# The beginning of a fused attention and mixture kernel rebuilt: how scales are spread, k ahead of q, both in halves

## The chip, the cores and the metric

One core of a Trainium2 chip runs the whole kernel. The metric is the device time of one execution in microseconds (us), as the median of several. Five engines work beside each other, each through its own list in order: TensorE (PE in the profile; matrix products and transposes, weight loads as PEld), VectorE (DVE), ScalarE (ACT), GpSimd (POOL) and SyncE (SP), which only issues transfers. They meet at semaphores alone.

## What is computed

For each of 4 batches of 512 tokens with 256 features, two adaptive layers follow each other. The modulation has six columns of features (shift, scale and gate for either layer).

```python
mod = (_silu(L0_c) @ L0_wmod).reshape(4, 6, 1, -1)
h = _layernorm(x) * (1 + ca) + sa
q, k, v = (h @ (codes * repeat(scales, 32, axis=0)) + bias  for each of q, k, v)   # 256 x 2048
attn = softmax(q @ k.T / sqrt(128))          # 16 heads of 128
x = x + ga * ((attn @ v) @ wo + bo)
h = _layernorm(x) * (1 + cb) + sb
x = x + gb * (h @ W.T + lora_of_the_two_best_of_8_experts(h))
```

The weights of q, k, v and o are stored as codes, and one scale holds for 32 rows of a column. For the change it matters that a scale has to reach the 32 partitions that hold its rows.

## The kernel before

The kernel is written engine by engine, and the order on each engine is the order of the text. Products are made with float32r numbers in two parts (high and low): `three` issues three products for one. So each operand needs a high part, made by ScalarE, and a low part, made by VectorE or GpSimd: h (`hT_hi`, `hT_lo`), the weights (`parts`), q, k, v, the probabilities (`pT_hi`, `pT_lo`) and the output of attention.

The 16 heads go in 8 pairs, and each pair runs 8 steps (2 heads for each of 4 batches), so there are 64 steps. `pair` stands once in every engine's list, and is called with `first=True` for steps 0 to 7, in a loop, and with `last=True`. In a step n TensorE makes the scores of n into four banks of PSUM (`score_ps`), the weighted sum of step n-2, the projections of q and k for step n+1, the output product, and the projection of v for n+1. VectorE makes the row maxima, 32x32 turns of the probabilities (`turn`, into `pB`), the low parts and the additions to `y_acc`. ScalarE makes the exponentials and high parts. SyncE moves the turned blocks by 16 transfers a step into `pT32` (L327), which starts when all four turns of the step are done (`pB_ok`). GpSimd makes the low parts of the probabilities (L404) and the weights of the next pair.

What comes ahead of step 0 is the place of the change:

- SyncE loads the condition, x of batch 0 (two halves), the modulation weights, then `load_first` for q and k: the codes and, in 4 transfers each (L291), the scales with every row read 32 times. x of batch 1, v, x of batch 2, o, x of batch 3 and the rest of the modulation weights follow.
- TensorE transposes the condition, keeps busy with 20 transposes of the unit matrix (L1111), makes the modulation columns of both chunks of features (L1117), transposes the normalised x of batch 0 (L1129), then 14 unit transposes more (L1136), the projection of q, that of k, and 10 unit transposes (L1164).
- VectorE makes the silu, the statistics of batch 0, its normalisation `z` (L805), the product of q's codes and scales (L843), the parts of h chunk by chunk (L811, L816), the biases and the statistics of batch 1.
- GpSimd makes the products for k and v (L377) and all `parts` of weights.
- ScalarE makes the exponential of the silu, the modulated h (`hT32`, L548), the high parts of q (L559) and k (L563), and normalises batch 1 (L586).

In step 0 VectorE's order is: four maxima (L941), turns 0 and 1 (L954), v's low part (L868), turns 2 and 3, the reciprocal, then the low parts of q (L857) and k (L862) for step 1 with the statistics of batch 2 in between, and the high parts of batch 1. `q_ok`, `k_ok` and `v_lo_ok` are what TensorE waits for.

## Time and profile before

| what | value |
|---|---|
| time, median of 3 runs | 777.58 us (777.32 to 777.62) |
| the profiled execution's own time | 777.42 us |
| its span | 775.5 us |
| busy: TensorE, VectorE, ScalarE, GpSimd | 766.5, 647.5, 517.6, 483.4 us |
| TensorE's granted clock, mean | 0.998 |
| transfers | 71898 packets, 90.67 MB |

The span is what the trace covers, from the first to the last recorded work. Times in the rows count from its start. A line of a timeline has the start, the time that the group took, the engine, the line of the kernel, the operation and its tiles (out<-in); "x4" means four instructions merged, and in brackets stands how long the engine had been idle and what ended that. TensorE's durations overlap, so from one start to the next is the better measure there.

### The profile page before, as it was taken

The page shows a single profiled execution, that of the slowest core. Times are in us where ns is not written, and L with a number is a line of the kernel's source. Part 1 is how long each engine was busy: PE and PEld are TensorE (multiplying, and loading weights), DVE is VectorE, ACT ScalarE, POOL GpSimd, SP SyncE. Part 2 cuts the span into 40 slices and gives each one's busy share as a digit, 9 for nine tenths or more (in the row PEclk, how much of TensorE's full clock was granted, in tenths as well). Part 3 has the DMA queues.
Part 4 walks back from the last instruction along what each step waited for, and adds up shares of the span by engine and source line. Part 5 has one row for each costly group of instructions (what it writes and reads, how often), then busy time and mean ns, then how long its engine had stood idle before and what let it go on. Part 6 is the DMA issues. An engine that isn't in the chain of part 4 may idle for free.

```text
span 775.5 us, 14722 instructions
## 1 busy us (share of the span) xinstructions
PE 766.5 (99%) x4206; PEld 667.7 (86%) x4206; DVE 647.5 (83%) x1254; ACT 517.6 (67%) x1124; POOL 483.4 (62%) x454
## 2 busy tenths in 40 slices
PE   7999999999999999999999999999999999999998
PEld 6888888888888888888888888888888888888887
DVE  5889888888888888888888888888898888879876
ACT  2788676667666676667666766676667676766841
POOL 4686576548655675556657575655667476789722
PEclk9999999999999999999999999999999999999999
DMA  7554355444454335444445434543355334433202
GB/s 216 162 154 124 95 147 150 139 107 99 118 144 131 95 96 139 129 124 98 110 133 147 98 94 122 146 125 95 96 145 152 95 94 107 112 89 86 56 1 109
DMA packets 71898, 90.67 MB, mean 117 GB/s; under 512 B 19574, under 2 KB 37431, under 8 KB 71867
## 3 DMA queue, kind: packets, MB, share of 16 engines
q1 hardware_dynamic: 53184, 74.00, 37.3%
q10 hardware_dynamic: 18682, 16.30, 7.0%
q8 instruction: 15, 0.25, 0.1%
q14 instruction: 17, 0.13, 0.1%
HBM read 22.06 MB, written 2.11 MB: 31 GB/s over the span
## 4 chain that ended last, share of the span: by engine, by line
PE 95%; POOL 1%; DVE 1%; DMA 1%; ACT 1%; SPq 1%; issue 0%; DVEq 0%
PE score L1102 9%; PE score L1103 9%; PE score L1104 9%; PE qv L1102 8%; PE qv L1103 8%; PE qv L1104 8%; PE o L1102 7%; PE o L1104 7%; PE o L1103 7%; PE ky L1102 4%; PE ky L1103 4%; PE ky L1104 4%; PE y L1102 2%; PE y L1104 2%; PE y L1103 2%; DMA stage<-in_L_attn_wk_scales_dram 1%
## 5 line engine op out<-in xcount | busy, mean ns | idle before, releaser
L404 POOL TENSOR_TENSOR pT_lo<-pT,pT_hi 128x512 fp32r<-128x512 f32 x248 | 314.6, 1305 | 240.7 <-ACT pT_hi L576 240.6
L660 ACT ACTIVATE prob<-score,neg_max 128x512 f32<-128x512 f32 x256 | 172.7, 688 | 79.7 <-DVE neg_max L941 79.5
L941 DVE TENSOR_REDUCE neg_max<-score 128x1 f32<-128x512 f32 x256 | 159.7, 682 | 1.6 <-PE score L1104 1.6
L954 DVE STREAM_TRANSPOSE pB<-prob 128x512 f32<-128x512 f32 x252 | 156.4, 678 | 0.0
L576 ACT ACTIVATE pT_hi<-pT 128x512 fp32r<-128x512 f32 x248 | 135.3, 620 | 0.0
L1102 PE MATMUL score<-k_hi,q_hi 128*128 128x512 f32 x256 | 101.2, 395 | 0.6 <-DVE k_lo L862 0.6
L1103 PE MATMUL score<-k_lo,q_hi 128*128 128x512 f32 x256 | 100.3, 392 | 0.0
L1104 PE MATMUL score<-k_hi,q_lo 128*128 128x512 f32 x256 | 99.7, 389 | 0.0
L1102 PE MATMUL o<-pT_hi,v_hi 128*128 128x512 f32 x248 | 96.6, 389 | 0.0
L1104 PE MATMUL o<-pT_hi,v_lo 128*128 128x512 f32 x248 | 96.5, 389 | 0.0
L1103 PE MATMUL o<-pT_lo,v_hi 128*128 128x512 f32 x248 | 96.5, 389 | 0.0
L857 DVE SCALAR_TENSOR_TENSOR q_lo<-qv,vecT,q_hi 128x512 fp32r<-128x512 f32 x64 | 47.9, 749 | 43.5 <-ACT q_hi L559 43.5
L862 DVE SCALAR_TENSOR_TENSOR k_lo<-ky,vecT,k_hi 128x512 fp32r<-128x512 f32 x64 | 48.0, 750 | 32.5 <-ACT k_hi L563 32.3
L559 ACT ACTIVATE q_hi<-qv,bias_now 128x512 fp32r<-128x512 f32 x64 | 44.2, 690 | 45.6 <-PE qv L1104 45.6
L563 ACT ACTIVATE k_hi<-ky,bias_now 128x512 fp32r<-128x512 f32 x64 | 44.2, 690 | 42.8 <-PE ky L1104 42.8
L1102 PE MATMUL qv<-wv_hi,hT_hi 128*128 128x256 f32 x252 | 71.6, 284 | 0.0
L1103 PE MATMUL qv<-wv_lo,hT_hi 128*128 128x256 f32 x252 | 71.3, 283 | 0.0
L1104 PE MATMUL qv<-wv_hi,hT_lo 128*128 128x256 f32 x252 | 71.3, 283 | 0.0
L571 ACT ACTIVATE o_hi<-o 128x512 fp32r<-128x512 f32 x63 | 37.8, 599 | 44.5 <-PE o L1104 42.3
L868 DVE TENSOR_TENSOR v_lo<-qv,v_hi 128x512 fp32r<-128x512 f32 x63 | 43.5, 691 | 27.2 <-ACT v_hi L567 27.0
L1104 PEld LDWEIGHTS score<-k_hi,q_lo 128*128 128x128 f32 x256 | 48.1, 188 | 10.5
L1102 PEld LDWEIGHTS score<-k_hi,q_hi 128*128 128x128 f32 x256 | 48.3, 189 | 9.1 <-issue 0.8
(262 smaller groups left out, 1824.7 us busy)
## 6 DMA issues: line engine op xcount, KB each, us to landing
pT<-pB SPq DMA_DIRECT2D x1008, 64.0 KB, 2.0
out_dram<-x_nat SPq DMA_DIRECT2D x8, 256.0 KB, 2.1
stage<-in_L_attn_wv_codes_dram ACTq DMA_DIRECT2D x7, 256.0 KB
stage<-in_L_attn_wv_scales_dram ACTq DMA_DIRECT2D x14, 128.0 KB
stage<-in_L_attn_wq_codes_dram ACTq DMA_DIRECT2D x7, 256.0 KB
stage<-in_L_attn_wq_scales_dram ACTq DMA_DIRECT2D x14, 128.0 KB
stage<-in_L_attn_wk_codes_dram ACTq DMA_DIRECT2D x7, 256.0 KB
stage<-in_L_attn_wk_scales_dram ACTq DMA_DIRECT2D x14, 128.0 KB
```

The source lines that it names most:

```text
L404: pool.tensor_tensor(split(pT_lo, kt), turned(par, kt), split(pT_hi, kt).bitcast(f32), ALU.subtract).then_inc(p_lo_ok, 1)
L559: act.activation(q_hi[:, :], qv_ps[:, :], ACT.Identity, bias=bias_now[:, 0, j:j + 1]).then_inc(q_hi_ok, 1)
L563: act.activation(k_hi[:, :], ky_ps[:, :], ACT.Identity, bias=bias_now[:, 1, j:j + 1]).then_inc(k_hi_ok, 1)
L576: act.activation(split(to, kt), turned(par, kt), ACT.Copy).then_inc(p_hi_ok, 1)
L660: act.activation(prob[:, i], score_ps[i][:, :], ACT.Exp, bias=neg_max[:, i:i + 1], accum_out=row_sum[:, s % 2, i:i + 1]).then_inc(exp_ok, 1)
L857: dve.scalar_tensor_tensor(out=q_lo[:, :], in0=qv_ps[:, :], scalar=bias[:, 0, head], in1=q_hi[:, :].bitcast(f32), op0=ALU.add, op1=ALU.sub ...
L862: dve.scalar_tensor_tensor(out=k_lo[:, :], in0=ky_ps[:, :], scalar=bias[:, 1, head], in1=k_hi[:, :].bitcast(f32), op0=ALU.add, op1=ALU.sub ...
L941: dve.tensor_reduce(neg_max[:, i:i + 1], score_ps[i][:, :], AX.X, ALU.max, negate=True).then_inc(max_ok, 1)
L954: dve.transpose(pB[:, s % 2, :, i].rearrange("p g k q -> p k g q"), prob[:, i].rearrange("p (k g q) -> p k g q", k=QT, g=G)).then_inc(pB_o ...
L1102: pe.matmul(dst, a_hi, b_hi, start=first, stop=False)
L1103: pe.matmul(dst, a_hi, b_lo, start=False, stop=False)
L1104: return pe.matmul(dst, a_lo, b_hi, start=False, stop=last)
```

## The change

The scales of q, k and v come as rows: `load_rows` on ScalarE's queue moves the 4 scale rows of each half of the features into 4 partitions of a tile that VectorE has zeroed (`rows_zero`), and TensorE spreads them over 128 partitions in PSUM by a product with a 0/1 matrix `block_rows` (`spread_rows`), padded with zeros to 128 partitions. VectorE multiplies codes and scales for all three, reading the scales from PSUM (`first_product`). SyncE loads k's codes ahead of q's.

The modulation is made chunk by chunk into two banks, and the transposes of a chunk follow directly, tile by tile behind `z`. The projections of k and then q are made in two halves of tokens, each half in its own bank (`project_halves`), with high and low parts by halves. Of the 44 unit transposes 6 stay. The high part of chunk 1 of h and the biases go from VectorE to ScalarE. Batch 1 is normalised by VectorE inside step 0 (was ScalarE, ahead of it). In step 0 VectorE's order is new, and all statistics of batch 2 come after the step.

```diff
+        block_rows = pB[:, 0, 1, 0]
+        scale_rows = dict(q=gb_row[:, 0:2], k=gb_row[:, 2:4],
+                          v=pB[:, 0, 0].rearrange("p i k q -> p (i k q)").rearrange("p (c n) -> p c n", c=2))
...
+        def load_rows(queue, m):
+
+            src = bass.AP(SCALES[m].tensor, 0, [[FEAT, NB], [NB * FEAT, 2], [1, PW]])
+            queue.wait_ge(rows_zero, 1 + "kqv".index(m))
+            queue.dma_start(scale_rows[m][0:NB], src).then_inc(ld_rows[m], 16)
...
+            load_first(sp, "k")
             load_first(sp, "q")
-            load_first(sp, "k")
             load_x(1)
...
             inverse_std(0)
+            parts("k", 0, 0)
             parts("q", 0, 0)
-            product("k", 0)
-            parts("k", 0, 0)
+            parts("v", 0, 0)
             parts("q", 0, 1)
             inverse_std(1)
-            product("v", 0)
-            parts("v", 0, 0)
             parts("k", 0, 1)
...
+            load_rows(act, "k")
+            load_rows(act, "q")
+            act.wait_ge(c_tr, 1)
+            act.activation(c_exp[:, :], qv_ps[:, 0:B * DC], ACT.Exp, scale=-1.0).then_inc(c_exped, 1)
+
+            load_rows(act, "v")
...
             for c in range(DC):
+                modulation_out(c)
                 input_high(0, c, score_ps[2 + c])
+            act.wait_ge(h_ev, 2)
+            act.activation(hT_hi[:, 1, tokens(0)], hT32[:, 1], ACT.Copy).then_inc(h0_hi, 1)
...
-            q_high(1, 0)
-            k_high(1, 0)
-            normalise(1, range(QT))
+            def half_high(m, u):
...
+            for m in "kq":
+                for u in range(2):
+                    half_high(m, u)
...
+            for m in "kqv":
+                dve.memset(scale_rows[m], 0.0).then_inc(rows_zero, 1)
+            dve.memset(block_rows, 0.0).then_inc(block_zero, 1)
...
+            first_product("k")
+            first_product("q")
+            input_hi(0, 0)
+            input_lo(0, 0)
+            dve.wait_ge(ld_x[1], 16)
+            row_statistics(1, 0)
+            row_statistics(1, 1)
+            input_lo(0, 1)
+            first_product("v")
+            row_statistics(1, 2)
+            row_statistics(1, 3)
             dve.wait_ge(vec_ok, 2)
...
+            half_low("k", 0)
+            half_low("k", 1)
+            half_low("q", 0)
+            half_low("q", 1)
+            variances(1)
...
+                    elif start:
+                        normalise(1, range(2))
+                        turn(0)
+                        v_low(1, 0, 0, ky_ps)
+                        normalise(1, range(2, QT))
+                        q_low(n + 2, head_slice(p, s + 1))
+                        turn(1)
+                        k_low(n + 2, head_slice(p, s + 1))
+                        turn(2)
+                        turn(3)
+                        inverse()
+                        input_hi(1, 0)
+                        input_hi(1, 1)
+                        dve.wait_ge(ld_x[2], 16)
+                        statistics(2)
...
-            for i in range(20):
+            for i in range(6):
                 pe.transpose(score_ps[0][:, (i % QT) * P:(i % QT + 1) * P], ident[:, :], ident[:, :])
+
+            def spread_rows(m):
+                pe.wait_ge(block_ok, 1)
+                pe.wait_ge(ld_rows[m], 16)
+                for c in range(2):
+                    ins = pe.matmul(first_scales(m)[:, c], block_rows[:, :, :].rearrange("a b q -> a (b q)"), scale_rows[m][:, c],
+                                    start=True, stop=True)
+                ins.then_inc(rows_mm[m], 1)
+
+            spread_rows("k")
+            spread_rows("q")
...
+            for u in range(DC):
+                for i, j in enumerate((SA + u, CA + u)):
+                    for c in range(DC):
+                        ins = pe.matmul(mod_banks[u][:, i * B:(i + 1) * B], wmod_1[:, c, j * P:(j + 1) * P], silu[:, c],
+                                        start=(c == 0), stop=(c == DC - 1))
+                ins.then_inc(mod_mm, 1)
+                for t in range(QT):
+                    pe.wait_ge(z_ok, t + 1)
+                    ins = pe.transpose(INPUT_BANKS[0][u][:, t * P:(t + 1) * P], z[:, 0, t, u * P:(u + 1) * P], ident[:, :])
+                ins.then_inc(h_tr, 1)
...
+            pe.transpose(score_ps[1][:, 0:VECS], vec_raw[:, :], ident[0:VECS, 0:VECS]).then_inc(vec_tr, 1)
+            spread_rows("v")
+
+            def project_halves(m, mm):
 
                 for c in range(DC):
-                    if by_half:
-                        pe.wait_ge(h_lo, c + 1)
+                    pe.wait_ge(h_lo, c + 1)
+                    cut = (slice(None), c, slice(0, HD))
+                    for u in range(2):
+                        ins = three(half_banks[m][u][:, 0:S // 2], (w_hi[m][cut], w_lo[m][cut]),
+                                    (hT_hi[:, c, half_tokens(u)], hT_lo[:, c, half_tokens(u)]), c == 0, c == DC - 1)
+                        if c == DC - 1:
+                            ins.then_inc((half_mm[m], mm)[u], 1)
...
+            pe.wait_ge(w_ok["k"], 1)
+            pe.wait_ge(mod_ok, 4)
+            project_halves("k", k_mm)
             pe.wait_ge(w_ok["q"], 1)
-            project(qv_ps, "q", 0, 0, True).then_inc(q_mm, 1)
-            pe.wait_ge(w_ok["k"], 1)
-            pe.wait_ge(mod_ok, 2)
-            project(ky_ps, "k", 0, 0).then_inc(k_mm, 1)
-            for i in range(10):
-                pe.transpose(score_ps[0][:, (i % QT) * P:(i % QT + 1) * P], ident[:, :], ident[:, :])
+            project_halves("q", q_mm)
```

## Rows read from the trace of the kernel before

**Rows 1.** The page, first part: busy time and share of each engine.
```profile
PE 766.5 (99%) x4206; PEld 667.7 (86%) x4206; DVE 647.5 (83%) x1254; ACT 517.6 (67%) x1124; POOL 483.4 (62%) x454
```

**Rows 2.** Three stretches: PE, PEld, DVE, ACT, POOL busy; granted clock, DMA share, GB/s.
```profile
7.50:10.75 3.25, 2.71 (x24) 2.46 (x23) 1.67 (x4) 0.58 (x3) 0.40 (x1) 1.00 0.57 156
11.00:14.25 3.25, 3.25 (x15) 3.25 (x16) 3.18 (x5) 0.87 (x2) 2.02 (x3) 0.51 0.98 252
14.25:17.75 3.50, 2.01 (x9) 1.31 (x9) 2.39 (x13) 0.89 (x2) 3.27 (x5) 1.00 0.73 248
```

**Rows 3.** Transfers: KB and us to landing; batch 1's x by issue; ScalarE's last vector.
```profile
stage<-in_L_attn_wq_codes_dram SPq DMA_DIRECT2D x1, 256.0 KB, 4.6
vec_raw<-in_L_attn_bv_dram ACTq DMA_DIRECT2D x1, 8.0 KB, 3.4
...
L309 SPq DMA_DIRECT2D x_nat<-in_L_attn_x_dram x1: 427/427/427, 7.8 to 7.8; - x1
...
DMA to landing us min/median/max: 7.8/7.8/7.8
```

**Rows 4.** Timeline of VectorE ahead of step 0.
```profile
7.93 1.67 DVE L805 SCALAR_TENSOR_TENSOR z<-x_nat,mv,rstd 128x256 f32<-128x256 f32 x4 [1.22 <-POOL rstd L362]
10.77 0.69 DVE L843 SCALAR_TENSOR_TENSOR stage<-stage 128x512 f32<-128x512 f32 x1 [1.17 <-DMA stage<-in_L_attn_wq_scales_dram]
11.38 0.42 DVE L811 CAST hT_hi<-hT 128x512 fp32r<-128x512 f32 x1
11.84 0.98 DVE L816 TENSOR_TENSOR hT_lo<-hT,hT_hi 128x512 fp32r<-128x512 f32 x1
...
15.64 1.41 DVE L783 BATCH_NORM_STATS2 stats<-x_nat 128x6 f32<-128x256 f32 x4 [1.04 <-DMA x_nat<-in_L_attn_x_dram]
```

**Rows 5.** Timeline of GpSimd and ScalarE ahead of step 0.
```profile
14.01 1.56 POOL L377 TENSOR_TENSOR stage<-stage 128x512 f32<-128x512 f32 x1 [0.60 <-DMA stage<-in_L_attn_wk_scales_dram]
...
16.34 0.73 POOL L390 TENSOR_TENSOR wk_lo<-stage,wk_hi 128x256 fp32r<-128x256 f32 x1
...
18.81 0.69 ACT L563 ACTIVATE k_hi<-ky,bias_now 128x512 fp32r<-128x512 f32 x1 [2.40 <-PE ky L1104]
```

**Rows 6.** Timeline of TensorE: first score products of steps 0 and 1.
```profile
20.43 0.47 PE L1102 MATMUL score<-k_hi,q_hi 128*128 128x512 f32 x1 [0.56 <-DVE k_lo L862]
...
30.60 0.40 PE L1102 MATMUL score<-k_hi,q_hi 128*128 128x512 f32 x1
```

**Rows 7.** Timeline of VectorE in steps 0 and 1, and TensorE's v of step 1.
```profile
21.40 2.75 DVE L941 TENSOR_REDUCE neg_max<-score 128x1 f32<-128x512 f32 x4 [1.11 <-PE score L1104]
24.06 1.29 DVE L954 STREAM_TRANSPOSE pB<-prob 128x512 f32<-128x512 f32 x2
25.98 0.69 DVE L868 TENSOR_TENSOR v_lo<-ky,v_hi 128x512 fp32r<-128x512 f32 x1 [0.62 <-ACT v_hi L567]
...
37.52 0.71 DVE L857 SCALAR_TENSOR_TENSOR q_lo<-qv,vecT,q_hi 128x512 fp32r<-128x512 f32 x1
...
38.71 0.37 PE L1102 MATMUL qv<-wv_hi,hT_hi 128*128 128x256 f32 x1
```

**Rows 8.** Step 0's probabilities: issues, landing time, first high part, low parts.
```profile
27.91 8.43 SPq L327 DMA_DIRECT2D pT<-pB  x13
...
pT<-pB SPq DMA_DIRECT2D x4, 64.0 KB, 2.0
...
40.69 0.64 ACT L576 ACTIVATE pT_hi<-pT 128x512 fp32r<-128x512 f32 x1
...
41.41 5.04 POOL L404 TENSOR_TENSOR pT_lo<-pT,pT_hi 128x512 fp32r<-128x512 f32 x4 [5.26 <-ACT pT_hi L576]
```

**Rows 9.** Timeline of TensorE and VectorE at the end of step 2.
```profile
51.60 0.28 PE L1102 MATMUL qv<-wv_hi,hT_hi 128*128 128x256 f32 x1
52.13 0.74 DVE L862 SCALAR_TENSOR_TENSOR k_lo<-ky,vecT,k_hi 128x512 fp32r<-128x512 f32 x1
53.04 0.40 PE L1102 MATMUL score<-k_hi,q_hi 128*128 128x512 f32 x1
```

More of the change, by code:

```diff
@@ L283, in load_first, with first_scales, half_tokens @@
                 rows = CODES[m].rearrange("(h p) d -> p h d", p=P)[:, 0:2]
-                at, row, half = [BLK * a for a in range(NB)], D, NB * D
             else:
                 rows = CODES[m].rearrange("(c p) f -> p c f", p=P)[:, :, 0:PW]
-                at, row, half = [BLK * a for a in range(NB)], FEAT, NB * FEAT
             queue.dma_start(codes[m][:, :, :], rows).then_inc(ld_w_first[m], 16)
-            for a in range(NB):
-                src = bass.AP(SCALES[m].tensor, a * row, [[0, BLK], [half, 2], [1, PW]])
-                queue.dma_start(scales[m][at[a]:at[a] + BLK], src).then_inc(ld_w_first[m], 16)
+            if m == "o":
+                for a in range(NB):
+                    src = bass.AP(SCALES[m].tensor, a * D, [[0, BLK], [NB * D, 2], [1, PW]])
+                    queue.dma_start(scales[m][BLK * a:BLK * (a + 1)], src).then_inc(ld_w_first[m], 16)
+        def load_rows(queue, m):
+            src = bass.AP(SCALES[m].tensor, 0, [[FEAT, NB], [NB * FEAT, 2], [1, PW]])
+            queue.wait_ge(rows_zero, 1 + "kqv".index(m))
+            queue.dma_start(scale_rows[m][0:NB], src).then_inc(ld_rows[m], 16)
+        def first_scales(m):
+            return {"q": o_ps[0], "k": o_ps[1], "v": score_ps[0]}[m][:, :].rearrange("p (c n) -> p c n", c=2)
+        mod_banks = (ky_ps, qv_ps)
+        half_banks = dict(q=(qv_ps, o_ps[0]), k=(ky_ps, o_ps[1]))
+        def half_tokens(u):
+            return slice(u * S // 2, (u + 1) * S // 2)
         def split(t, kt):
@@ L393, in input_lo @@
                 for c in range(DC):
[L394 to L395 removed]
+                    if b == 1:
+                        pool.wait_ge(h_hi, c + 2)
                     else:
@@ L798, in statistics, with normalise @@
                 variances(b)
-            def normalise(i):
+            def normalise(i, tiles=range(QT)):
                 b = i % B
                 dve.wait_ge(ln_rstd, i + 1)
-                for t in range(QT):
+                for t in tiles:
                     dve.scalar_tensor_tensor(out=z[:, b % 2, t], in0=x_nat[:, b * QT + t], scalar=mv[:, b, t, 0:1],
@@ L813, in input_lo @@
             def input_lo(b, c):
-                dve.wait_ge(h_hi, DC * b + c + 1)
+                if c:
+                    dve.wait_ge(h0_hi, 1)
+                else:
+                    dve.wait_ge(h_hi, 1)
                 dve.tensor_tensor(hT_lo[:, c, tokens(b)], hT32[:, c], hT_hi[:, c, tokens(b)].bitcast(f32),
@@ L970, in pair @@
                         turn(1)
-                        if start:
-                            v_low(1, 0, 0, ky_ps)
                         turn(2)
@@ L1296, in pair @@
                     early = first and s < 2
-                    pe.wait_ge(q_ok, n + 1)
-                    pe.wait_ge(k_ok, n + 1)
+                    if start:
+                        pe.wait_ge(half_lo["k"], 1)
+                        pe.wait_ge(k_ok, 1)
+                        pe.wait_ge(vec_ok, 2)
+                    else:
+                        pe.wait_ge(q_ok, n + 1)
+                        pe.wait_ge(k_ok, n + 1)
                     for i in range(QT):
+                        if start and i % 2 == 0:
+                            pe.wait_ge((half_lo["q"], q_ok)[i // 2], 1)
                         if not start:
```

107 lines of the change are left out of this document (50 added, 57 removed).

## The prediction

> **What bounds the kernel now.** I read the page's busy shares first. TensorE works 99% of the span [rows 1], so a saving counts only where TensorE itself is late, and that is the beginning. The timeline of the beginning shows why. The scales of q, spread by 32-fold reads from memory, hold VectorE's first product until 10.77 [rows 4], and those of k hold GpSimd's until 14.01 [rows 5]. After k's product (1.56 us) come its parts and its projection; ScalarE makes the high part from 18.81 in 0.69 us [rows 5], VectorE the low part, and the first scores start at 20.43, those of step 1 at 30.60 [rows 6]. From there TensorE hardly pauses, but a gain at 20.43 reaches the end only if nobody behind it is late in turn. So the last views are those of the other engines in steps 0 to 2: how much slack do they have?
>
> Little. VectorE's low part of q for step 2 runs from 37.52 to 38.23, and TensorE goes on to v, which needs it, at 38.71 [rows 7]: slack 0.5. The probabilities of step 0 are moved by 16 transfers of SyncE, which start at 27.91, right behind VectorE's last turn; 13 are issued in 8.43 us (0.65 apart), so the sixteenth at 37.65, and a transfer lands 2.0 after its issue [rows 8]. All have landed at 39.65, and ScalarE makes their high parts from 40.69 [rows 8]: slack 1.04. From that instant on, VectorE's work of step 2 is a chain without a gap; its low part of k ends at 52.87, and step 3's scores need it at 53.04 [rows 9]: slack 0.17. So TensorE's gain lasts only as far as step 0's probabilities come earlier too.
>
> **The change part by part.**
> (a) Scales. SyncE issues 12 transfers fewer for q, k and v (8 ahead of batch 1's x); three small ones on ScalarE's queue take their place. The codes of k take q's place, whose landing was 4.6 behind the issue at 2.57, so 7.2 [rows 3]; q's follow at about 9. For the rows of scales the nearest transfers are ScalarE's vectors, the latest of which landed 3.4 after its issue [rows 3]. VectorE's zeroing ahead of them has no row: between 0.2, little more than nothing, and 0.69, its 512-wide product [rows 4]; I take 0.6, the latter being nearest in size. Three of them put k's issue at 1.4 and q's at 2.0, landing by 4.8 and 5.4. The spreading products of TensorE have no row either: 256 columns cost 0.12 in one pass [rows 9], so two products cost 0.24 at least and, with several passes at half the clock, up to some 1.8; I take 1.7. They take the place of 14 of 20 warm-up transposes ahead of the modulation. If q's end 0.6 behind the modulation weights' landing, the wait for z covers it.
> (b) VectorE. z ends at 7.93+1.67 = 9.6 [rows 4]; ScalarE has fewer issues ahead of the exponential, so 9.5. Then k's product 0.69 (10.2), q's 0.69 (10.9), high part of chunk 0, 0.42 (11.3; it waits for nothing, because the transposes of chunk 0 now follow z tile by tile), low part 0.69 to 0.98 [rows 4] (12.2), two statistics of 0.35 (12.9), low part of chunk 1 (13.7). ScalarE makes the high part of chunk 1 by 12.4, in time.
> The two statistics stand behind a new wait, for x of batch 1, with chunk 1's low part, v's product and all low parts of k queued behind it. Before, this x was issued at 7.8 and landed 7.8 later, 15.6 [rows 3]. Now it is issued at 3.5, behind 1.5 MB instead of 2. The landing of q's codes shows 1.25 MB in the 6.0 us from 1.2 to 7.2 [rows 3]; the 0.75 MB more (k's or q's codes and this x) take 3.6 at that rate: 10.8, ahead of 12.2. I take no wait.
> (c) GpSimd loses the products of k and v. k's parts (0.73 for the low one [rows 5], up to 0.3 more beside VectorE) are done by 11.9, q's by 13.3. Neither is late.
> (d) TensorE and its clock. v's spreading stands ahead of k's projection, about 11.0 to 12.7. The clock is the open cost. After the stretch 7.50 to 10.75, small products and transposes with 2.71 us busy, it was granted at 0.51 in 11.00 to 14.25, that is at 1.2 GHz. Behind that stretch, which was filled with transposes, it was back at 1.00, and it stayed there in 14.25 to 17.75 with only 2.01 of 3.50 us busy [rows 2]. The change leaves the first stretch as thin, but fills the second with v's spreading and k's projection, and the third is busier than before; so I expect the same pattern, slow from about 11 to 14 and 2.4 GHz behind it.
> The Trainium skill, "TensorE: Matmul & The Clock Gate", Part 4, says that transposes don't count as busy for the gate. By that rule the dropped transposes cost nothing and rival C has no ground; by rows 2 the clock rose behind little else than transposes, so the trace doesn't agree, and C keeps its chance.
> Twelve half-width products take 53.04-51.60 = 1.44 us [rows 9]. k's chunk 0 is hidden behind VectorE; chunk 1 runs 13.8 to 14.6, q's projection to 16.1, its first half done at 15.7. ScalarE's high part of a half costs between 0.35 (half of 0.69) and 0.69, 0.48 taken because part of the 0.69 is fixed; VectorE's low part the same. With 0.3 to 0.5 of handing over the first scores are at **17.2**, 3.2 earlier.
> (e) Step 0 on VectorE. z of batch 1 moves here from ScalarE: 1.67 [rows 4]. Up to the last turn there are four maxima 2.75, z 1.67, four turns of 0.645, the low parts of v 0.69, q 0.71 and k 0.74: 9.1 [rows 7, 9]. The first maximum starts 0.97 behind the first scores [rows 6, 7], and ScalarE's high parts of v and k cost some 0.3 of waiting. Last turn: 17.2+0.97+9.1+0.3 = 27.6, where it was 27.9. **Of 3.2 us, 0.3 is left at the turns**, for z and two low parts now stand ahead of them.
> (f) TensorE in steps 0 and 1. v's low part ends at 17.2+0.97+2.75+0.84+0.65+0.69 = 23.1; from there to step 1's scores it took 30.60-26.67 = 3.9 [rows 6, 7], so 27.0: 3.6 earlier. But VectorE now has in one block, from 27.6 on, the reciprocal 0.1, the high parts of batch 1 0.84, statistics of batch 2 2.1, v's low part 0.7, maxima and turns 2.5 each, reciprocal and q's low part 0.8: 37.1 at most (36.8 if short ones overlap), where it was 38.23. TensorE, 3.6 ahead with 0.5 of slack, waits there for some 2 us and keeps 1.7 to 1.9.
> (g) Step 0's probabilities. SyncE starts 0.3 earlier and all have landed at 39.35. ScalarE is free then, its modulation copies ahead of them following TensorE, and takes them at 39.35 instead of 40.69. GpSimd's low parts (5.04, from 0.7 behind [rows 8]) and VectorE's chain of step 2 follow by the same 1.3. SyncE has no pause up to step 1's last transfer and lands that only 0.3 earlier, which is just enough for ScalarE; from step 3 on everything moves alike.
>
> **The sum.** 0.3 at the turns and 1.04 of slack at the landing: **1.3 us**. The profiled execution took 777.42, a span of 775.5 and 1.9 around it, 0.16 below the median of 777.58. The span becomes 774.2, the time by the median **776.2**. Each 1 us at the first scores is 1 us here.
>
> **The rivals.**
> A. The forecast, 776.2 (775.4 to 777.0, first scores 0.8 either way). For it: the slacks of 1.04 and 0.17. Chance 0.55.
> B. The lead is kept: VectorE's pieces fit into its waits, or the first scores come near 16. Up to 3.5, 774.1. Against it: z adds 1.67 to a chain whose slack is 0.5. Chance 0.2.
> C. The clock doesn't come back at 14.3 without the 24 dropped transposes behind z. k's last chunk costs 0.7 more and q's projection 1.4, less 0.4 behind its first half; first scores 18.9, gain -0.4, 778.0. Chance 0.15.
> D. Slower: the wait for x of batch 1. If it lands at 15.6 as before, 3.4 behind VectorE's readiness at 12.2, the first scores are at 20.6, the last turn at 31.0, the landing at 42.75, where ScalarE took it at 40.69: 2.1 slower, 779.6. It costs from a landing at 12.2 on and turns the sign at 13.5. Chance 0.1.
>
> **How the numbers follow.** Under 0.2% (1.55 us) a measurement here can hardly tell a difference. Of A, 0.22 lies beyond 1.55 us; with B faster is 0.42. The rest of A (0.33) and C make the same 0.48. D is slower, 0.1. The range 774.3 to 778.2 takes in A, C and B down to near its end; it leaves out D and B's last part.
>
> **What would show it.** First scores near 17.2 at a clock of 1.00; the last turn of step 0 and SyncE's first move near 27.6; TensorE idle for about 2 us in step 1 for q's low part, and for some tenths in step 2 for VectorE or the probabilities. VectorE waiting for x behind 12.2 would mean D, a clock of 0.5 behind 14.3 C, a last turn ahead of 26.5 B.

## The result, and the profile after

The changed kernel takes **779.07 us** (median of 11; 777.06 to 781.72) where the kernel before, beside it, takes 777.62 (777.30 to 778.26). The ratio is 1.0022, interval 1.0013 to 1.0030: slower by 0.2%. The prediction of 776.2 was wrong in sign. And the times now spread over 4.7 us, where those of before spread over 1.0 here, and over 2.4 in the largest set of its executions (34, beside the run again). (Four single executions of over 1000 us, two of them of the kernel before, are left out of all ranges and medians.)

The profiled execution took 778.99, with a span of 777.2. First the page of the changed kernel:

```profile
span 777.2 us, 14702 instructions
PE 766.4 (99%) x4192; PEld 666.8 (86%) x4192; DVE 652.2 (84%) x1264; ACT 517.1 (67%) x1127; POOL 479.8 (62%) x450
```

TensorE's share is unchanged [rows 1], so the difference must again be sought where TensorE is late. Next, the windows of the beginning, in the columns of [rows 2]:

```profile
6.50:9.75 3.25, 1.92 (x14) 1.49 (x13) 2.07 (x5) 0.05 (x1) 1.03 (x1) 1.00 1.06 372
10.00:13.25 3.25, 3.25 (x16) 2.83 (x15) 2.78 (x6) 1.45 (x4) 2.97 (x4) 0.50 1.06 323
13.25:16.75 3.50, 3.50 (x14) 3.14 (x14) 2.29 (x5) 1.34 (x5) 1.06 (x2) 0.50 1.05 287
```

The granted clock is 0.50, that is 1.2 GHz, in two stretches; before it was slow in one and back at 1.00 in 14.25 to 17.75 [rows 2]. TensorE's timeline shows what ran in them:

```profile
8.61 1.05 PE L1201 MATMUL ky<-c_silu,y_acc 128*128 128x4 f32 x8 [1.33 <-DMA y_acc<-in_L_wmod_dram]
10.05 1.71 PE L1201 MATMUL qv<-c_silu,y_acc 128*128 128x4 f32 x8
12.92 2.07 PE L1189 MATMUL score<-pB 128*128 128x256 f32 x4
15.22 0.41 PE L1176 MATMUL ky<-hT_hi,wk_lo 128*128 128x256 f32 x1
15.43 0.41 PE L1174 MATMUL y<-hT_hi,wk_hi 128*128 128x256 f32 x1
19.50 0.47 PE L1174 MATMUL score<-k_hi,q_hi 128*128 128x512 f32 x1 [0.82 <-DVE q_lo L918]
```

The modulation weights landed 6.5 after their issue instead of 4.9, v's spreading took 2.07, and k's half-width products follow at 0.21 instead of 0.12. First scores at 19.50: 0.9 earlier than before [rows 6], 2.3 later than predicted. Now the other engines in steps 0 to 3, from their timelines:

```profile
12.77 0.74 DVE L826 BATCH_NORM_STATS2 stats<-x_nat 128x6 f32<-128x256 f32 x2
29.04 1.29 DVE L1024 STREAM_TRANSPOSE pB<-prob 128x512 f32<-128x512 f32 x2
30.36 0.61 SPq L351 DMA_DIRECT2D pT<-pB  x1
42.25 0.63 ACT L607 ACTIVATE pT_hi<-pT 128x512 fp32r<-128x512 f32 x1 [0.53 <-DMA pT<-pB]
54.55 0.43 PE L1174 MATMUL score<-k_hi,q_hi 128*128 128x512 f32 x1
```

VectorE finds x of batch 1 without a wait (rival D is out). The last turn of step 0 ends at 30.33, SyncE starts 2.45 later than before, ScalarE takes the high parts 1.56 later, now waiting for the landing [rows 8], and step 3's scores start 1.51 later [rows 9]. That is the whole difference of the medians (1.45).

One more observation carries much of what follows. In the profiled executions the scores of step 3 start 722.4 to 722.7 before the end of the span, in 12 of the 16 kernels here, before and after among them. In the other four (hold, fill_all, fill_z, late4) it is 723.1 to 723.4, and in just these ScalarE waits 1.30 to 1.65 for the landing of step 1's probabilities at about 52. So the start of step 3's scores, plus what is left of a wait of that length, sets the time (fill1's 0.77 costs nothing).

### The profile page after: what moved, and what is told of

Its sections match the earlier page's. It is cut to its first block, busy times and chain, and to the rows that moved or that the text cites. A ratio compares the mean times of both kernels' runs of the same rounds, so it can differ in the third digit from the quotient of the medians.

```text
span 777.2 us, 14702 instructions
## 1 busy us (share of the span) xinstructions
PE 766.4 (99%) x4192; PEld 666.8 (86%) x4192; DVE 652.2 (84%) x1264; ACT 517.1 (67%) x1127; POOL 479.8 (62%) x450
## 4 chain that ended last, share of the span: by engine, by line
PE 90%; DVE 4%; ACT 2%; SPq 1%; DMA 1%; POOL 1%; issue 1%; DVEq 0%
PE score L1174 9%; PE score L1175 9%; PE score L1176 9%; PE qv L1174 7%; PE qv L1175 7%; PE qv L1176 7%; PE o L1174 7%; PE o L1175 7%; PE o L1176 7%; PE ky L1174 4%; PE ky L1176 4%; PE ky L1175 4%; PE y L1176 2%; PE y L1174 2%; PE y L1175 2%; SPq L351 1%
```

## The experiments

All times of one row come from one profiled execution of that kernel, except for the median and the range. "Landed" is ScalarE's first high part of step 0's probabilities, "wait 1" its wait for those of step 1. A median stands for 10 to 12 executions, in z_act for 6 and in z_hi_act for 8; the kernel before was measured beside each set, 125 times in all.

| kernel | median (range) | first scores | SyncE's start | landed | wait 1 | scores of step 3 |
|---|---|---|---|---|---|---|
| before | 777.6 to 777.7 (776.6 to 779.5) | 20.43 | 27.91 | 40.69 | 0 | 53.04 |
| changed | 779.07 (777.1 to 781.7) | 19.50 | 30.36 | 42.25 | 0.16 | 54.55 |
| again | 779.65 (777.8 to 781.9) | 17.23 | 28.57 | 40.28 | 0 | 53.77 |
| hold | 778.91 (776.9 to 781.5) | 17.45 | 28.31 | 39.95 | 1.65 | 52.30 |
| fill_t | 778.87 (776.8 to 780.1) | 17.22 | 28.55 | 40.06 | 0 | 53.73 |
| fill_m | 778.17 (776.7 to 779.1) | 18.68 | 29.55 | 41.06 | 0 | 54.76 |
| fill1 | 778.37 (777.1 to 780.2) | 19.57 | 30.49 | 42.00 | 0.77 | 54.33 |
| fill_all | 777.30 (776.8 to 777.9) | 16.67 | 28.00 | 39.71 | 1.50 | 52.01 |
| turns | 777.16 (776.5 to 777.5) | 17.28 | 24.93 | 40.36 | 0 | 52.72 |
| bare | 777.95 (777.2 to 781.8) | 21.19 | 28.18 | 40.96 | 0 | 53.31 |
| late2 | 777.59 (777.1 to 779.2) | 20.05 | 28.20 | 40.31 | 0 | 52.67 |
| late4 | 778.58 (777.6 to 779.1) | 20.66 | 29.65 | 41.52 | 1.32 | 53.84 |
| z_act | **775.53** (774.9 to 775.8) | 17.23 | 24.89 | 38.77 | 0 | 51.13 |
| z_hi_act | 775.72 (775.5 to 776.1) | 17.87 | 25.52 | 39.40 | 0 | 51.76 |
| z_plain | 778.03 (774.8 to 780.9) | 19.48 | 27.08 | 40.75 | 0 | 53.13 |
| fill_z | 777.20 (776.0 to 777.9) | 17.72 | 28.09 | 40.03 | 1.30 | 52.37 |

### The beginning: landing or clock?

**again** is the changed kernel unaltered.

> The changed kernel itself once more, to see its spread and a second profile. Clock theory (T1): its times lie anywhere from 777 to 782 because TensorE's clock drops to 1.2 GHz in the beginning at another moment in each execution; the profile then shows first scores and the last turn of step 0 moving with the slow stretch, about 1 us for 1 us in the time. Rival (T2, transfers): the spread comes from when the modulation weights land (8.6 us in the profile of the changed kernel); then the clock's stretch would be the same and the landing another.

779.65, ratio 1.0022 (1.0011 to 1.0033). This execution was another one than the first: the clock is 1.00 from its first rise at 8.7 on (how that is read stands at z_plain below), and the first scores start at 17.23, as predicted, although the modulation weights landed nearly as late as in the first profile (6.3 behind their issue; the modulation began 0.15 earlier). So the clock is what costs most of the 2.3 there. (The landing isn't free: where the clock is kept, the first scores follow it from 8.1 on, 16.67 in fill_all with the modulation begun at 8.09, 17.23 in z_act with 8.33, 17.87 in z_hi_act with 9.00.) And yet this execution took 778.15, 0.8 less than the first profiled one and still some 2 more than predicted, and the median is no better. Its windows show why:

```profile
10.00:13.25 3.25, 3.05 (x21) 2.40 (x21) 2.69 (x5) 2.66 (x8) 3.09 (x4) 1.00 1.06 325
34.80:38.20 3.40, 2.68 (x17) 2.35 (x18) 2.93 (x6) 3.40 (x10) 0.00 (x0) 1.00 0.40 99
38.20:42.50 4.30, 4.30 (x28) 4.30 (x26) 2.61 (x10) 3.12 (x10) 1.51 (x2) 0.64 0.55 150
```

The clock fell later instead, in steps 1 and 2 (0.50 from about 39.4 to 42.8), behind a stretch in which TensorE waits 0.7 at a time and makes small modulation products. In TensorE's timeline, from v's projection to the scores of step 3:

```profile
37.78 0.39 PE L1174 MATMUL qv<-wv_hi,hT_hi 128*128 128x256 f32 x1 [0.72 <-DVE q_lo L924]
53.77 0.40 PE L1174 MATMUL score<-k_hi,q_hi 128*128 128x512 f32 x1
```

37.78 is 0.93 earlier than before [rows 7], 53.77 is 0.73 later than before.

**hold** keeps the queue free until the modulation weights have landed.

```diff
             load_first(sp, "q")
+            sp.wait_ge(ld_wmod, 16)
             load_x(1)
             load_first(sp, "v")
```

> The changed kernel, but SyncE waits for the modulation weights before it issues x of batch 1 and all that follows. T2 (crowding: seven large transfers issued within 4.6 us delay the modulation weights from 7.0 to 8.6 us): they land near 7.1, the transposes of chunk 1 and h follow 1.5 us earlier and the time falls by 1 to 1.5 us, to about 777.5. T1 (clock): the landing moves but the slow stretch still holds the projections of k and q, gain under 0.7 us, and the spread of the times stays some 4 us wide.

778.91, ratio 1.0016 (1.0006 to 1.0026), and the spread of 4.5 stays. The weights landed 6.0 behind their issue, not 4.9, and 6.0 is also what fill_all has without this wait. So crowding by the transfers issued behind q's codes isn't shown to delay the landing, and it explains hardly any of the time. In the profile the clock was slow for 3.4 us only, and yet ScalarE waits 1.65 for step 1's probabilities.

**fill_t** puts 6 unit transposes, **fill_m** two real products of 256 columns, into TensorE's wait for the modulation weights.

```diff
             spread_rows("q")
+            for i in range(6):
+                pe.transpose(score_ps[0][:, (i % QT) * P:(i % QT + 1) * P], ident[:, :], ident[:, :])
             pe.wait_ge(ld_wmod, 16)
```

```diff
             spread_rows("q")
+            for c in range(2):
+                pe.matmul(first_scales("v")[:, c], block_rows[:, :, :].rearrange("a b q -> a (b q)"), scale_rows["q"][:, c],
+                          start=True, stop=True)
             pe.wait_ge(ld_wmod, 16)
```

> The changed kernel with six unit transposes more between the spreading of q's scales and the wait for the modulation weights, where TensorE was idle 1.3 us. T1, with transposes counting as activity: the clock no longer falls at 10 us, the projections of k and q run at 2.4 GHz, the first scores come near 17.5 instead of 19.5, the time is about 777.0 and its spread shrinks below 1 us. If transposes do not hold the clock, it stays at 779 with the same spread. T2: no change in the time.

> The same place filled with two products of 256 columns (the spreading of q's scales repeated, its result is overwritten) instead of transposes. T1: if only real products hold the clock, this one comes to about 777.0 with a small spread and the one with transposes does not; if both hold it they are alike; at half clock the fill takes some 1.7 us, so the modulation may start 0.4 us late. T2: no change, or 0.3 us slower.

778.87 (ratio 1.0011, 1.0002 to 1.0019) and 778.17 (1.0005, 0.9996 to 1.0014). The 777.0 that I had expected of one or both didn't come. fill_t's profile has the beginning at 1.00 and first scores at 17.22, but 0.50 at 39.2 to 42.6; fill_m's has a slow stretch in both places, in the beginning from 12.8 to 16.2. Filling one place doesn't keep the other.

**fill1** fills step 1 instead, with six products of 512 columns into a bank that is free, and **fill_all** does both.

```diff
+            def keep_busy(count):
+                for _ in range(count):
+                    pe.matmul(o_ps[0][:, :], w_hi["q"][:, 0, 0:HD], hT_hi[:, 0, tokens(0)], start=True, stop=True)
...
                     if first and s == 1:
                         pe.wait_ge(ld_wmod2, 16)
                         pe.wait_ge(h_ev, DC * 2)
                         modulation_columns(0)
+                        keep_busy(3)
...
+                        if first and s == 1:
+                            keep_busy(3)
                         pe.wait_ge(q_ok, n + 2)
```

> The changed kernel with 3 products of 512 columns on TensorE in step 1 behind the first modulation columns, and 3 more ahead of its wait for VectorE's low part of q, where it stood idle 0.7 us each time (results unused). Dip theory (T3): in the second profile of the changed kernel the clock was at 1.2 GHz from 39.3 to 42.7, behind a stretch of waits and small products, and v, transposes and scores took 4.6 us from 37.8 on where the kernel before needed 3.2; so 1.4 us of the gain are given back there in many executions. With the fill the clock stays at 1.00 in steps 1 and 2 and the median falls by 0.7 to 1.4 us against the changed kernel, the slowest executions (781 to 782) stay. Rival (T1 alone, the beginning): no gain, as the beginning is untouched; 0.2 to 0.6 slower if the fill delays the projections.

> The fill in step 1 and the two products of 256 columns behind the spreading of q's scales together. T1 and T3 together: median 776.5 to 777, slowest below 778.5. If crowding of transfers were the cause of the spread, it would stay as wide as with neither.

fill1: 778.37 (1.0009, 1.0000 to 1.0018), 1.2 GHz at 9.2 to 16.0, none in step 1. fill_all: **777.30** (0.9995, 0.9986 to 1.0004), 0.3 above the range that I had expected, and the spread is 1.1. Six added products in step 1, some 1.6 us (in turns, below, 0.80 and 0.77 from the first of three to what follows), on an engine that is busy for 99% of the time, and two more ahead of it make the kernel 1.8 us faster and steady. The profile has no slow stretch behind the first rise, and the mean clock on record is 1.000 in all eleven executions, where the 22 of the changed kernel have 0.991 to 0.998. So the clock explains the slower median and nearly all of the spread. (The changed kernel and fill_all were not measured beside each other; against the kernel before beside each, the difference is 1.7, or 2.2 with again.) But first scores at 16.67 are 3.8 earlier than before, and of that 0.3 is left at the end, with an interval that includes zero. This is the next question.

**bare** asks the same of the kernel before: it leaves out the 14 and the 10 unit transposes behind z (L1136, L1164).

> The kernel before with the 14 and the 10 unit transposes behind the first input's transposes taken out, nothing else. T1: without them the clock stays low through the projections of q and k in many executions, median 0.5 to 1.5 us slower, spread 2 to 4 us as in the changed kernel. Rival (the transposes don't count for the clock): no change beyond 0.1 us.

777.95, where the kernel before beside it has 777.56; three of the ten executions took over 780, and the ratio is 1.0015 (1.0002 to 1.0027). The mean clock on record is 0.995 or less in seven of the ten and in none of the 114 executions of the kernel before in these rounds, which have 0.996 to 1.000. The windows of bare:

```profile
10.00:13.25 3.25, 2.04 (x9) 1.55 (x8) 2.08 (x4) 1.80 (x4) 1.34 (x2) 0.50 0.99 211
13.25:16.75 3.50, 3.05 (x6) 1.81 (x7) 3.43 (x8) 0.21 (x1) 3.15 (x4) 0.50 0.85 258
```

Without them the clock stays at 1.2 GHz from 9.5 to 19.7, where it was back by 14.25 [rows 2] and, in the profiles of late2 and late4 below, which keep the transposes, by 15.7 and 13.2. The first scores start at 21.19. The Trainium skill, "TensorE: Matmul & The Clock Gate", Part 4, says that a transpose doesn't count as busy for the gate. The trace doesn't agree: unit transposes held the clock up here.

### From the first scores to the end: what took the rest?

In fill_all, ScalarE's high parts of step 0 and step 1, and TensorE's start of step 3:

```profile
39.71 0.63 ACT L607 ACTIVATE pT_hi<-pT 128x512 fp32r<-128x512 f32 x1 [0.37 <-DMA pT<-pB]
51.48 0.63 ACT L607 ACTIVATE pT_hi<-pT 128x512 fp32r<-128x512 f32 x1 [1.50 <-DMA pT<-pB]
52.01 0.42 PE L1174 MATMUL score<-k_hi,q_hi 128*128 128x512 f32 x1
```

Step 3's scores came 1.03 earlier than before, but then ScalarE waited 1.50 for step 1's probabilities. SyncE had issued all 32 transfers of steps 0 and 1 one behind the other, from 28.00 on, without waiting for VectorE; step 1's are taken 23.5 behind that start, in hold (28.31, 51.85), fill_z (28.09, 51.58) and late4 (29.65, 53.08) too. So the end of step 0's last turn bounds both landings.

But 23.5 isn't the least that they take. SyncE's first 26 issues in fill_all and in fill_t:

```profile
28.00 18.27 SPq L351 DMA_DIRECT2D pT<-pB  x26
28.55 16.73 SPq L351 DMA_DIRECT2D pT<-pB  x26
```

One issue of step 1 took 1.94 in fill_all where most take 0.59. fill_z and late4 have such an issue too (1.76 to the next), and in hold the last transfer landed 3.3 behind its issue instead of 2.0. In fill_t, with neither, the last one landed 21.9 behind the first issue, and in the changed kernel's first profile 22.3. So by these numbers about 1.35 (1.94 less 0.59) of the 1.50 in fill_all's profile is one slow issue, and without it the landing would have been just in time. Such an issue, 1.1 to 2.0 to the next, stands in step 1 of 10 of the 16 profiles; what makes it slow isn't shown.

**turns** moves that end. It is fill_all with all four turns of step 0 together, ahead of z of batch 1 and the low parts of q and k.

```diff
                     elif start:
-                        normalise(1, range(2))
                         turn(0)
                         v_low(1, 0, 0, ky_ps)
-                        normalise(1, range(2, QT))
-                        q_low(n + 2, head_slice(p, s + 1))
                         turn(1)
-                        k_low(n + 2, head_slice(p, s + 1))
                         turn(2)
                         turn(3)
+                        normalise(1)
+                        q_low(n + 2, head_slice(p, s + 1))
+                        k_low(n + 2, head_slice(p, s + 1))
```

> As fill_all, but VectorE makes the four turns of step 0 ahead of the normalisation of batch 1 and the low parts of q and k, so that SyncE starts some 3 us earlier. Landing theory (T4, my step g): the probabilities of step 0 set when step 3's scores start, 12.3 us behind ScalarE's first high part; with the turns first that comes as early as ScalarE's modulation copies allow, and the time falls by 0.4 to 0.8 us against fill_all. Rival (T5: VectorE's total of steps 0 and 1 is the bound): no change within 0.2 us, TensorE waiting longer for z and for q's low part.

777.16, ratio 0.9994 (0.9985 to 1.0003): no better than fill_all, as the rival said. SyncE starts at 24.93, 3.1 earlier, and no landing is waited for. But TensorE now waits for what was put off:

```profile
26.51 0.66 PE L1219 MATMUL o<-ident,z 128*128 128x128 f32 x4 [1.63 <-DVE z L854]
40.16 0.18 ACT L732 ACTIVATE modT<-y 128x16 f32<-128x16 f32 x1 [1.02 <-PE y L1301]
52.72 0.40 PE L1173 MATMUL score<-k_hi,q_hi 128*128 128x512 f32 x1
```

ScalarE in turn waits 1.02 for TensorE's modulation columns, ahead of the high parts. From 26.51 on TensorE works without a gap up to step 3. VectorE's list is too long whichever piece stands last.

**z_act** therefore takes z away from VectorE: it is turns with z of batch 1 on ScalarE, two tiles ahead of q's high part and two behind it (the first two hunks below are ScalarE's list, the last VectorE's; GpSimd makes the shift for it, as in the kernel before). **z_hi_act** moves the two high parts of batch 1's input to ScalarE as well.

```diff
                     if start:
                         v_out(1, 0, 0, ky_ps)
+                        normalise(1, range(2))
...
                         q_high(n + 2, (s + 1) % 2)
+                        if start:
+                            normalise(1, range(2, QT))
...
                         turn(3)
-                        normalise(1)
```

> As the run turns (full-size products kept on TensorE, all four turns of step 0 together), but with the normalised rows of batch 1 made by ScalarE, two ahead of q's high part and two behind it, as in the kernel before, instead of by VectorE (4 products, 1.63 us). In the run turns TensorE waits 1.63 us for these rows at 26.5 us and then works without a gap up to the scores of step 3. Theory T7 (the rows on VectorE, behind the turns, are what the first gap is made of): the input's transposes start at 25.0 to 25.7 instead of 26.51, scores of step 3 at 51.8 to 52.2 instead of 52.72, total 776.1 to 776.6, ratio to the kernel before 0.9985. Rival T6 (the landing of step 1's probabilities, behind 32 transfers without a pause, gives it back as in the run fill_all): 777.0 to 777.3. Rival T5 (VectorE's high parts of batch 1 and its statistics, still there, hold step 1's maxima): 776.9 to 777.1.

> As z_act, and with the two high parts of batch 1's input made by ScalarE too (2 more copies of about 0.6 us there, 2 fewer on VectorE, which in the run turns lost 2.0 us between 28.02 and 30.02 us to them and to their waits). Theory T5 (VectorE's total in steps 0 and 1 is the bound left): step 1's maxima start 1 to 1.5 us earlier than in turns (32.53), scores of step 3 at 51.2 to 51.8, total 775.8 to 776.3. Theory T7: TensorE's own work from 25 us on is the bound, so no more than z_act gives (within 0.2 us of it). Rival T6 (landing of step 1's probabilities, or of the modulation weights' second part): 777.0 or above, with TensorE waiting for low parts of the probabilities in steps 2 and 3.

z_act: **775.53** (6 executions), ratio 0.9969 (0.9957 to 0.9981), 2.1 faster than before and 3.5 than the changed kernel, with a range of 0.9. z_hi_act: 775.72 (0.9974, 0.9963 to 0.9984), the same within its interval. z_act's timelines:

```profile
24.91 0.66 PE L1218 MATMUL o<-ident,z 128*128 128x128 f32 x4
38.77 0.64 ACT L607 ACTIVATE pT_hi<-pT 128x512 fp32r<-128x512 f32 x1
49.04 0.62 ACT L607 ACTIVATE pT_hi<-pT 128x512 fp32r<-128x512 f32 x1
51.13 0.40 PE L1175 MATMUL score<-k_hi,q_hi 128*128 128x512 f32 x1
```

The transposes start 1.60 earlier than in turns, a little more than expected, and step 3's scores 1.59 earlier. From 24.91 on TensorE doesn't pause and no landing is waited for, so VectorE's total no longer binds; that is why z_hi_act brings nothing more. T7 holds; I had put z_act at 776.1 to 776.6, half a microsecond too cautious.

**fill_z** asks whether z alone was the culprit: fill_all with z on ScalarE, and the change's own order of turns.

> As the run fill_all (changed kernel with the clock kept up, 777.3), with z of batch 1 moved back from VectorE to ScalarE; VectorE keeps the change's order: one turn, v's low part, q's low part, one turn, k's low part, two turns. Theory (z on VectorE is the step that took the gain, 1.63 us of VectorE's chain up to the last turn): last turn of step 0 ends at 26.2 to 26.6 instead of 27.97, probabilities of both steps land in time, scores of step 3 at 50.8 to 51.5, total 775.3 to 776.0, within 0.4 us of z_act. Rival (the turns behind the low parts hold SyncE, and its 32 transfers without a pause bound the landing of step 1's probabilities as in fill_all): total 776.3 to 777.0, with ScalarE waiting 0.5 us or more for the landing in step 3.

777.20, ratio 0.9991 (0.9982 to 1.0000): within 0.1 of fill_all. My theory fell, the rival held. VectorE's timeline of step 0 says why:

```profile
24.43 0.75 DVE L927 SCALAR_TENSOR_TENSOR q_lo<-qv,vecT,q_hi 128x512 fp32r<-128x512 f32 x1 [0.86 <-ACT q_hi L590]
26.10 0.75 DVE L932 SCALAR_TENSOR_TENSOR k_lo<-ky,vecT,k_hi 128x512 fp32r<-128x512 f32 x1 [0.30 <-ACT k_hi L594]
26.77 1.29 DVE L1027 STREAM_TRANSPOSE pB<-prob 128x512 f32<-128x512 f32 x2
```

Where z was, VectorE now waits 0.83 for ScalarE's high part of v and 0.86 and 0.30 for those of q and k, and two turns stand behind those low parts. ScalarE makes two tiles of z (22.70 to 23.81) just ahead of q's high part. The last turn starts at 26.77, in fill_all at 26.68. Neither edit pays alone (turns and fill_z are each 0.1 us ahead of fill_all), both together 1.8.

**z_plain** is z_act without any added product on TensorE.

> The changed kernel with z of batch 1 on ScalarE and all four turns of step 0 together, as the run z_act, but without any of the additional full-size products on TensorE (two of 256 columns ahead of the modulation, six of 512 columns in step 1). Clock theory: stretches at 1.2 GHz come back, in the beginning, in step 1, or both, at a place that varies between executions; median 776.5 to 778, spread over 2 us, slower than z_act (775.5) by 1 us or more. Rival (the order of step 0 alone was the cause, and the products only cost their 1.5 us in a stretch in which TensorE has no pause): median 774.5 to 775.6, spread below 1.5 us.

778.03, ratio 1.0003 (0.9989 to 1.0017), and a range of 6.1 us, from 774.78, the fastest execution of all, to 780.86. The clock theory holds on this order too: the added products are worth 2.5 us of the median, because they keep the clock. The profiled execution shows something more:

```profile
13.25:16.75 3.50, 3.50 (x17) 2.88 (x16) 2.49 (x6) 1.77 (x5) 0.12 (x1) 1.00 1.03 327
13.69 2.07 PE L1190 MATMUL score<-pB 128*128 128x256 f32 x4
15.76 0.28 PE L1176 MATMUL ky<-hT_lo,wk_hi 128*128 128x256 f32 x1
```

The record says 1.00 throughout, yet v's spreading took 2.07, as in the changed kernel at 0.50. From about 15.5 on the products follow at 0.12. In z_act the same spreading took 1.13, and the same kind of work had become fast much earlier, ahead of 7.3 (k's scales, then the added products):

```profile
4.13 2.04 PE L1190 MATMUL y<-gb_row,pB 128*128 128x256 f32 x4
7.25 1.03 PE L1197 MATMUL score<-gb_row,pB 128*128 128x256 f32 x4
11.28 1.13 PE L1190 MATMUL score<-pB 128*128 128x256 f32 x4
```

So the executions begin at 1.2 GHz, although the windows have 1.00 there, and what differs is when the clock rises first. The trace's own list of clock changes begins with that rise: at 15.7 in z_plain, at 6.8 in z_act, and at 6.5 and 8.7 in the two profiles of the changed kernel. The executions of the kernel before fit this: the 17 with a mean of 1.000 on record have the longer spans, 776.3 by the median against 775.5 of the other 97.

### How much slack had the landing?

**late2** and **late4** are the kernel before with two or four tiny transfers ahead of step 0's sixteen.

```diff
                     sp.wait_ge(pB_ok, QT * (n + 1))
+                    if first and s == 0:
+                        for i in range(2):
+                            sp.dma_start(scratch[0:B * DC, 832 + 48 * i:880 + 48 * i],
+                                         cond.rearrange("b (c p) -> (b c) p", p=P)[:, 0:48]).then_inc(ld_pad, 16)
```

> The kernel before, with two tiny transfers (96 partitions by 192 bytes or less, into a corner that nothing uses) issued by SyncE ahead of step 0's sixteen probability transfers, so that these start about 0.9 us later (two issues of 0.4 to 0.45 us) and nothing else changes. Theory T6 (the landing of step 0's probabilities has about 1.04 us to spare before ScalarE's high parts, as the slack in the kernel before says): ScalarE takes the high parts at the same time, scores of step 3 within 0.2 us, total within 0.3 us of the kernel before (777.6 to 777.9). Rival (SyncE's ten microseconds of issues per step bind the following steps, so a late start is passed on whole): 778.3 to 778.5, ratio about 1.0011.

> The kernel before, with four such tiny transfers ahead of step 0's probability transfers: these start about 1.8 us later. Theory T6: the slack of about 1.04 us is used up, high parts of step 0's probabilities and the scores of step 3 come 0.7 to 0.9 us later, total 778.3 to 778.5 (ratio 1.001). Rival (passed on whole from the first): 779.2 to 779.4, ratio 1.0023. Rival (probabilities' landing never binds, only VectorE and TensorE do): 777.6, ratio 1.0.

An issue cost 0.33 instead of the 0.4 to 0.45 that I had assumed, so the sixteen start 0.7 and 1.4 behind the last turn. That turn itself ends 0.4 earlier than in the kernel before in late2's profile and 0.4 later in late4's, so their start moves by 0.3 and by 1.7. late2: 777.59, ratio 1.0000 (0.9991 to 1.0009), high parts at 40.31, without a wait. late4: 778.58, 1.0010 (1.0001 to 1.0019):

```profile
29.65 15.83 SPq L332 DMA_DIRECT2D pT<-pB  x24
41.52 0.63 ACT L582 ACTIVATE pT_hi<-pT 128x512 fp32r<-128x512 f32 x1 [0.32 <-DMA pT<-pB]
53.84 0.42 PE L1108 MATMUL score<-k_hi,q_hi 128*128 128x512 f32 x1
```

SyncE 1.74 later, high parts 0.83 later, scores of step 3 0.80 later. With the slack of 1.04 it should be 0.70. The step on which the prediction's sum rests is right to 0.1. The whole execution is 1.4 longer than the profiled one before, not 0.8, because ScalarE then waits 1.32 for step 1's probabilities; by the medians the difference is 0.9.

## Why the prediction was wrong, step by step

**What bounds the kernel** held. A saving counted only through TensorE's lateness, and the landing of step 0's probabilities has the slack read from the profile (late2, late4). What came on top of it is in (d), (e) and (g).

**(a) and (b)** The landing of the modulation weights was mis-sized: 6.5 (6.0 to 7.2 in the runs) instead of 4.9, which I had taken over unchanged. It puts the end of chunk 1's low part at 13.95 in again (it starts at 13.28 and takes 0.67), where I had 13.7 and where fill_all, with the earliest landing, has 13.39. From there to the first scores it took 3.28 in both, where I had 3.5. The two errors cancel. x of batch 1 landed ahead of 12.77, as forecast, and D was wrong.

**(c)** held as far as it goes: TensorE waits for none of GpSimd's parts of the weights here. What GpSimd's work beside VectorE costs is in (e).

**(d) is the step that failed.** I said: slow from about 11 to 14, then 2.4 GHz. With the clock at 1.00 the first scores came at 17.23 and 17.22 (again, fill_t). In the first profile it was slow from 9.9 to 16.8, and that cost most of the 2.3 by which the first scores are late, where the whole miss is 2.9. Rival C named this mechanism and its cause, the dropped transposes, and bare shows the cause on the kernel before. I gave it 0.15 because one trace showed one recovery. But one trace is one draw: profiles of the changed kernel and of its neighbours have the slow stretch in the beginning, in step 1, in both or from the start. "TensorE: Matmul & The Clock Gate", Part 1, of the Trainium skill says that the point at which the clock rises varies between executions of one kernel. The traces agree: the first rise is at 6.5 in one execution of the changed kernel and at 8.7 in the other, and at 15.7 in z_plain, whose beginning has the same products. I should have taken that as a cost in the median and a wider range, also for step 1, where the prediction didn't look for the clock at all. There the 2 us of waits that step (f) itself forecast help to make the stretch thin.

**(e)** From first scores to the end of the last turn I had 10.4 us (17.2 to 27.6); it is 10.8 in the changed kernel and 11.3 in again. The largest part of it is z itself. VectorE's z in the changed kernel, GpSimd's work beside it, and VectorE's z in turns:

```profile
23.12 1.54 DVE L854 SCALAR_TENSOR_TENSOR z<-x_nat,mv,rstd 128x256 f32<-128x256 f32 x2
25.78 0.85 DVE L854 SCALAR_TENSOR_TENSOR z<-x_nat,mv,rstd 128x256 f32<-128x256 f32 x2
22.68 1.29 POOL L401 TENSOR_TENSOR stage<-stage 128x512 f32<-128x512 f32 x1
24.82 1.63 DVE L854 SCALAR_TENSOR_TENSOR z<-x_nat,mv,rstd 128x256 f32<-128x256 f32 x4
```

The first tile of z took 1.14 in the changed kernel and 1.62 in again and fill_all, where each of the other three takes about 0.46. In all seven profiles with z ahead of the first turn it runs beside this product of GpSimd and ends 0.28 to 0.29 behind it; in turns, where it doesn't meet one, it takes 0.44. So z cost 2.2 (2.7 in again), not 1.67. That GpSimd's product holds it up is read from this coincidence; no run moves the product alone. The second part is ScalarE's high part of k, for which VectorE waits 0.46. fill_z shows how much lies in such waits: with z gone from VectorE they fill its place. Of the queued pieces I summed the durations, not the arrivals.

**(f)** I forecast a wait of some 2 us for q's low part. The changed kernel has three waits, 0.71 and 0.73 for v's low parts and 0.70 for q's, 2.1 together. Right in sum, wrong in place.

**(g)** That step 1's transfers land 0.3 earlier, "which is just enough for ScalarE", holds only if each issue takes its usual time: it leaves nothing to spare. With first scores early, step 1's landing is what is late: 1.50 in fill_all, 1.65 in hold, most of it behind one slow issue or one slow landing. In fill_all's profile it took back most of the 1.0 won at step 3's scores. Had the clock held, the changed kernel would have come out at about 777.3 (fill_all), inside the range given but short of 776.2.

**What makes the median 1.5 slower**, then: some 1.8 us from the clock (changed kernel against fill_all), less the 0.3 (its interval includes zero) that the rebuilt beginning yields with its order of step 0. With the other order it yields 2.1 (z_act). What the executions at 781.7 had isn't settled: no profile caught one. A slow start as in z_plain's profile together with a slow stretch in step 1 would fit, but that is argued, not shown. The record's mean clock, 0.998 for two of the three slowest, neither shows nor excludes a slow start. Nor is it settled why eight executions of fill_m with a mean of 1.000 on record still spread from 776.67 to 779.06, while the eleven of fill_all, which has the same beginning, stay within 1.1.

## What to carry to other kernels

Before removing filler work from an engine whose clock depends on its activity, look at every thin stretch, the ones that the saving creates further on included, and count the times' spread as part of the result: a kernel that is 2 us shorter on paper lost 2.5 us of its median for want of eight idle products. When work is moved ahead of a step that other engines wait for, follow each piece's inputs and not only its duration; here the order of VectorE's list and the engine that makes z had to change together, and each alone showed nothing. A lead at the start is worth what the tightest later hand-over leaves of it, and where a queue issues two steps' transfers one behind the other, look at the second step's landing, which one slow issue can make late.

## What the runs showed of the hardware

- The clock fell to 1.2 GHz while TensorE was never idle for more than 1.33 us at a time: behind 6.50 to 9.75 with 1.92 of 3.25 us busy, and behind 34.80 to 38.20 with 2.68 of 3.40.
- Unit transposes held the clock up (slow until 19.7 in bare, until 14.2, 15.7 and 13.2 in the three profiles that keep them).
- The granted clock of the record can't be trusted ahead of the first change that it notes: it is 1.00 in z_plain, with products at half rate until about 15.5. Durations of like products tell.
- An issue of SyncE that mostly takes 0.59 took 1.94 in the midst of fill_all's 32.
- VectorE's first tile of z took 1.14 to 1.62 instead of 0.46 beside a 128x512 product of GpSimd, and ended 0.28 to 0.29 behind it, in seven profiles of seven.
- The same transfer, of the modulation weights, landed 4.9 to 5.7 us behind its issue in the kernel before and its variants, and 6.0 to 7.2 in the changed kernel and its variants, hold among them (6.0). Why isn't shown.
